# Feed-forward stage: VectorE's statistics and normalising, and GpSimd's closing sum, at other places in their queues; the local-attention loop written out

## The reference

```python
def _layer(x, wqkv, qs, ksc, wo, lg, lb, w1, b1, w2, b2):
    h = shift_token(x)                        # half of the columns from the token before
    q, k, v = jnp.split(h @ wqkv, 3, axis=-1) # 8 heads of 64
    q, k = rotary_xpos(l2norm(q) * qs, l2norm(k) * ksc)
    o = local_attention(q, k, v)              # a window of 128 and the one before it
    x = x + o @ wo
    h = shift_token(x)
    h = (h - mean(h)) / jnp.sqrt(var(h) + 1e-05) * lg + lb
    a, g = jnp.split(h @ w1 + b1, 2, axis=-1) # 682 each
    return x + (a * gelu(g)) @ w2 + b2
...
y = xn
for l in range(2):
    y = _layer(y, wqkv[l], ...)
out = x + s * silu(y)
```

## Time and profile before

| | |
|---|---|
| median of three runs | 1978.15 us (1977.71 to 1978.39) |
| the profiled execution's own time | 1978.07 us |
| its span (first to last instruction) | 1976.2 us |
| busy: PE / PEld / DVE / ACT / POOL | 93% / 66% / 76% / 61% / 50% |
| window phases | about 631 to 1073 us and 1292 to 1725 us |
| feed phases | about 1075 to 1290 us and 1727 to 1976 us |

### The profile page before, as it was taken

The page is one execution under the profiler, slowest core; times in us unless marked ns, Lnnn a source line. Parts: engine busy times, 40 slices in busy tenths (PEclk is TensorE's granted clock), DMA queues, the critical chain, the costliest instruction groups (busy, mean ns, idle before and its releaser), DMA issues. The chain is left out here.

```text
span 1976.2 us, 38537 instructions
## 1 busy us (share of the span) xinstructions
PE 1839.4 (93%) x12768; PEld 1314.2 (66%) x12768; DVE 1502.2 (76%) x4131; ACT 1208.0 (61%) x2523; POOL 988.4 (50%) x801
## 2 busy tenths in 40 slices
PE   6879999999998899999997899979999999789999
PEld 5723333333333687878886788868888888668888
DVE  5778888888881998989996555369999999855654
ACT  3516666666666677777775433447777777644553
POOL 3532223222222777767773433357777777443433
PEclk9969999999998899999998999989999999989999
DMA  6993456456430000000022112110000001232222
GB/s 208 308 194 44 66 68 84 60 74 78 59 44 23 14 28 24 25 28 28 28 74 69 61 57 65 44 35 24 26 27 27 27 27 28 63 117 85 71 69 86
DMA packets 142299, 126.87 MB, mean 64 GB/s; under 512 B 31091, under 2 KB 124719, under 8 KB 141999
## 3 DMA queue, kind: packets, MB, share of 16 engines
q1 hardware_dynamic: 140782, 123.36, 27.2%
q10 hardware_dynamic: 1344, 1.31, 0.2%
HBM read 82.41 MB, written 41.96 MB: 63 GB/s over the span
## 5 line engine op out<-in xcount | busy, mean ns | idle before, releaser
L659 ACT ACTIVATE ca_pr<-ca_pS 128x1024 f32<-128x1024 f32 (+3 forms) x384 | 296.6, 811 | 207.2 <-PE ca_pS L573 166.6
L488 POOL TENSOR_SCALAR_AFFINE_SELECT ca_pr<-ca_pr 128x256 f32<-128x256 f32 x256 | 103.7, 409 | 372.9 <-ACT ca_pr L659 368.8
L687 DVE CUSTOM_DVE_ANT_0 ca_masked<-ca_pR,ca_later 128x256 f32<-128x256 f32 (+3 forms) x512 | 235.9, 485 | 43.2 <-PE ca_pR L549 39.4
L549 PE MATMUL ca_pR<-ca_ks,ca_qs 96*128 96x512 bf16 (+3 forms) x768 | 220.6, 345 | 9.1 <-DVEq L743 5.7
L573 PE MATMUL ca_pS<-ca_qs,ca_ks 98*128 98x512 bf16 (+3 forms) x768 | 184.8, 332 | 10.5 <-issue 5.3
L691 DVE TENSOR_REDUCE ca_mx<-ca_pR 128x1 f32<-128x512 f32 x256 | 175.7, 686 | 24.8 <-PE ca_pR L549 23.0
L549 PEld LDWEIGHTS ca_pR<-ca_ks,ca_qs 96*128 96x128 bf16 x768 | 70.7, 98 | 165.0 <-DVE ca_mx L687 90.6
L909 POOL TENSOR_TENSOR wb_tsn<-wb_qk,wb_tab 128x512 f32<-128x512 f32 x62 | 133.4, 2173 | 71.1 <-DVE wb_pn L1127 71.1
L594 PE MATMUL ca_pO<-ca_pr,ca_va 128*32 128x512 f32 (+3 forms) x1536 | 166.0, 504 | 1.2 <-POOL ca_pr L488 0.8
L909 POOL TENSOR_TENSOR w_tsn<-w_qk,w_tab 128x512 f32<-128x512 f32 x62 | 129.0, 2101 | 76.0 <-DVE w_pn L1127 67.3
L985 ACT ACTIVATE w_pe<-w_sm,w_nmax 128x256 f32<-128x256 f32 (+1 forms) x256 | 123.2, 483 | 66.7 <-DVE w_nmax L1117 66.4
(11 more groups left out here) (293 smaller groups left out, 5417.7 us busy)
## 6 DMA issues: line engine op xcount, KB each, us to landing
QKP<-p_parts SPq DMA_DIRECT2D x32, 384.0 KB, 5.2
ca_qs<-QKP SPq DMA_DIRECT2D x96, 128.0 KB, 6.5
ca_ks<-QKP SPq DMA_DIRECT2D x96, 128.0 KB, 7.0
w_xt<-X SPq DMA_DIRECT2D x64, 128.0 KB, 2.1
X<-w_x SPq DMA_DIRECT2D x64, 128.0 KB, 1.7
f_hh<-X SPq DMA_DIRECT2D x32, 256.0 KB, 6.2
p_xin<-x SPq DMA_DIRECT2D x8, 512.0 KB, 5.7
X<-p_xn SPq DMA_DIRECT2D x8, 512.0 KB, 4.9
```

The source lines that it names most:

```text
L549: pe.matmul(bank[:, 0:w], qs[0:SHIFT_ROW, u, h, i * P:(i + 1) * P], ks[0:SHIFT_ROW, u, h, k0:k0 + w], start=True, stop=True).then_inc(ring ...
L659: act.activation(pr[:, k % 2, pair, :, 0:w], pS[:, pair, :, 0:w], ACT.Exp, scale=CS).then_inc(p_ready, 1)
L687: dve.tensor_tensor_reduce(masked[:, jb % RING, 0:w], pR[jb % RING][:, 0:w], later[:, 512 - w:512], -1.0, BIG, ALU.add, ALU.min, mx[:, i, ...
```

## The change

1. In the window phase `steps` writes out all 32 tiles on every engine; no hardware loop is left.
2. In the feed phase VectorE computes the moments of block s + 2 in three pieces: two `bn_stats` after chunk 0, two after chunk 1, `bn_aggr` after chunk 2. Its normalising moves to `residual`, two instructions ahead of each of the last two results.
3. SP loads the rows of block s + 3 in step s, a block earlier, into the buffer that block s + 1 has left.
4. In the closing phase GpSimd's `gated_sum` moves from the head of a step to behind the second `low`.
5. Block 0 and step 1: ScalarE's high part of w2 comes after block 0 and VectorE's low part after chunk 2 of block 1; TensorE turns block 2 after `up(1)` instead of ahead of it and waits for w2 only there; VectorE's and ScalarE's parts of turning block 2 move with it; block 2's moments come after chunk 4 and its normalising at the end of block 0.

VectorE in layer 0's feed phase, block 0 before, from its chunk 3 to the turned block 2's low part (`f_af` the product, `f_tlo` the turned block's low part, `f_stt`/`f_mv` the moments, `f_hn` the normalised rows, `f_w_lo` w2's low part, `f_ahi` the short chunk's low part).

The core of the diff:

```diff
@@ phase_window
-    def steps(e, step):
-        with e.Fori(0, NW // TPB - 1) as it:
-            for j in range(TPB):
-                step(it * TPB + j, j, it)
-        for j in range(TPB):
-            step(NW - TPB + j, j, NW // TPB - 1)
+    def steps(step):
+        for w in range(NW):
+            step(w, w % TPB, w // TPB)
...
@@ phase_feed, sync
-            sp.wait_ge(S["hn_ready"], ONE + g0 + 1)
-            load_h(sp, F, layer, X, 2, 0)
+            for i in range(2):
+                sp.wait_ge(S["hn_ready"], ONE + g0 + i + 1)
+                load_h(sp, F, layer, X, 2 + i, i)
...
             def step(s, j, it):
-                if within(s, 2) is not None:
-                    sp.wait_ge(S["hn_ready"], ONE + g0 + s + 1)
-                    load_h(sp, F, layer, X, s + 2, j)
+                if within(s, 3) is not None:
+                    sp.wait_ge(S["hn_ready"], ONE + g0 + s + 2)
+                    load_h(sp, F, layer, X, s + 3, 1 - j)
...
@@ phase_feed, gpsimd
             def body(s, j, it):
 
                 for ch in range(WHOLE):
                     low(s, j, ch)
-                    if ch == 1 and within(s, 2) is not None:
+                    if ch == 1 and closing and s >= 3:
+                        gated_sum(s - 3)
+                    if ch == (1 if s else WHOLE - 1) and within(s, 2) is not None:
                         rstd_of(s + 2, j)
...
                 add_b2(s - 1, 1 - j, it - 1 + j)
-                if closing and s >= 3:
+                if closing and s == NS:
                     gated_sum(s - 3)
                 step(s, j, it)
...
@@ phase_feed, scalar
-            def midway():
-                turned(1, 1)
-                act.wait_ge(S["w_loaded"], ONE + (layer + 1) * 4 * 16)
-                act.activation(w2_hi[:, :, :], w2_st[:, :, :], ACT.Copy).then_inc(S["w_hi"], 1)
-
-            gelus(0, 0, midway)
+            gelus(0, 0, lambda: turned(1, 1))
+            act.wait_ge(S["w_loaded"], ONE + (layer + 1) * 4 * 16)
+            act.activation(w2_hi[:, :, :], w2_st[:, :, :], ACT.Copy).then_inc(S["w_hi"], 1)
 
             def step(s, j, it):
-                if within(s, 1) is not None:
+                if s > 1 and within(s, 1) is not None:
                     turned(s + 1, 1 - j)
                 if within(s, 0) is not None:
                     gelus(s, j)
+                if s == 1:
+                    turned(s + 1, 1 - j)
...
@@ phase_feed, vector (residual, body, block 0, step)
                 for n in range(SUP):
+                    if n >= 2 and within(s, 3) is not None:
+                        normalise(s + 3, 1 - j, n - 2)
                     if n == SUP - 1 and within(s, 1) is not None:
                         tail_low(s + 1, 1 - j)
...
-                        if ch == 2:
-                            moments(s + 2, j, it + 1)
-                        elif ch == 3:
-                            normalise(s + 2, j, it + 1)
+                        if ch < 2:
+                            stats(s + 2, j, it + 1, ch)
+                        elif ch == 2:
+                            means(s + 2, j)
+                    if s == 1 and ch == 2:
+                        dve.wait_ge(S["w_hi"], ONE + 4 * layer + 4)
+                        dve.tensor_tensor(w2_lo[:, :, :], w2_st[:, :, :], w2_hi[:, :, :].bitcast(F32), ALU.subtract)\
+                           .then_inc(S["w_split"], 1)
...
-            for ch in range(2, HC):
+            for ch in range(HC):
                 gated(0, 0, ch)
-                if ch == WHOLE - 1:
-                    dve.wait_ge(S["w_hi"], ONE + 4 * layer + 4)
...
-                if ch == 2:
-                    moments(2, 0, 1)
-                elif ch == HC // 2:
+                if ch == HC // 2:
                     lo_of(1, 1)
-                    normalise(2, 0, 1)
+                elif ch == WHOLE - 1:
+                    for half in range(2):
+                        stats(2, 0, 1, half)
+                    means(2, 0)
             tail_low(0, 0)
+            for half in range(2):
+                normalise(2, 0, half)
...
@@ phase_feed, tensor
             up(0, 0, midway)
-            pe.wait_ge(S["w_split"], ONE + 4 * layer + 4)
-            pe.sem_inc(K.passed, 1)
 
             def step(s, j, it):
-                if within(s, 1) is not None:
+                if s > 1 and within(s, 1) is not None:
                     turn(s + 1, 1 - j)
                 if within(s, 0) is not None:
                     up(s, j, lambda: turn_a(s - 2) if closing and s >= 2 else None)
+                    if s == 1:
+                        turn(s + 1, 1 - j)
+                        pe.wait_ge(S["w_split"], ONE + 4 * layer + 4)
```

74 lines of the change are left out of this document (38 added, 36 removed).

## The result

The changed kernel took 1954.89 us, the median of four runs (1951.79 to 1957.08), beside 1977.93 us of the kernel before in the same session. The ratio is 0.9889, with a 95% interval from 0.9873 to 0.9905: 22 us, or 1.1%, faster. The forecast was 1954.5.

What follows compares the result with a forecast made beforehand. TensorE, busy 93% of the span, bounds the kernel, so only its pauses or slow clock can be won. 6.6 + 9.1 + 4.0 + 0.3 + 3.6 = 23.6 us off 1978.07 gives 1954.5 us, range 1950 to 1959 (62%).

Steps and rivals of the forecast that it cites:

- Part 1: Window phase, layer 0: two loop edges each lose 3.29 us when written out, 6.6 us; nothing in layer 1.
- Rival 1: Window phase: loop-edge pauses come back where written-out code jumps or streams; price 6.6, 1961.1 us; 9%.
- rival 5: TensorE's 32 formerly looped tiles: late fetches at 3.29 us each; from 8 on slower, 1981 us; 3%.
- Rival 4: Layer 1's two looped edges: a hidden delay of 3.29 us on each goes too, 1947.9 us; 1%.
- Part 2: Layer 0's feed phase, blocks 2 to 5: the pause in `down`'s third tile goes whole, 9.1 us.
- Part 3: Closing phase, blocks 3 to 6: 28.10 us a block for 29.10 with the sum moved, 4.0 us.
- The margin of the third low part: Closing blocks: low part done 15.3 us after the turning, needed at 17.0 for chunk 4's product; 1.7 spare.
- rival 2: Step 1 or each block: larger or new pauses, part 3 at nothing, part 4 lowest; 1960.1 us; 11%.
- Part 4: Block 0 and step 1: new waits replace old; gains 0.3 us in layer 0, 3.6 in the closing phase.
- the pause ahead of chunk 2: Block 1: TensorE pauses 2.2 us, VectorE being held for most of its low part by GpSimd's bias add.
- What the clock would do: Step 1: slow matmuls behind two pauses over 2.1 us cost 0 to 3.4 us, taken as 2.6.
- rival 3: Step 1: the clock stays up, new pauses being shorter or broken up; 2 x 2.6 more, 1949.3 us; 12%.

Runs made afterwards that it cites:

- loop_out_only: The kernel before with only the window's loops written out, feed-forward phase as it was; 1971.26 us, ratio to before 0.9973.
- pad192: The kernel before with 192 semaphore increments added at the start of TensorE's queue; 1995.62 us, a single run.
- the pads: The kernel before with 64, 128 or 192 semaphore increments added at the start of TensorE's queue; single runs of 1983.59, 1994.52 and 1995.62 us.
- both_back: The changed kernel with VectorE's moments again behind chunk 2 and normalising behind chunk 3, the earlier row load kept; 1968.08 us, ratio to before 0.9945.
- loops_back: The changed kernel with the window's loops put back as loops; 1960.28 us, ratio to before 0.9913.
- sum_back: The changed kernel with GpSimd's closing sum again at the head of its step; 1959.39 us, ratio to before 0.9904.
- turn_mid: The changed kernel with block 2 turned in the middle of block 1's up product rather than after it; 1947.98 us, ratio to before 0.9846.
- bias_later: The changed kernel with GpSimd's bias add of block 0 moved behind its second low part of block 1; 1952.63 us, ratio to before 0.9869.
- pad128: The kernel before with 128 semaphore increments added at the start of TensorE's queue; 1994.52 us, a single run.
- three_moves: The changed kernel with block 2 turned mid block 1, block 0's bias add behind block 1's first low part, woc's low part behind block 0's residual; 1939.26 us.
- pad64: The kernel before with 64 semaphore increments added at the start of TensorE's queue; 1983.59 us, a single run.

## Why the prediction was right, step by step

- **Part 1, 6.6 us.** The two edges gave 2 x (28.15 - 24.85) = 6.6. Rival 1 (the pause moves) and rival 5 (late fetches in written-out code) are out, by the tile ends, by loop_out_only and by the seven packets a round that came without a wait. Why layer 1 gained nothing was open in the prediction; the shifts and the packets show it: its code lay where a round was not fetched again. Rival 4 asked for four edges. The rule of the Trainium skill ("Runtime: NRT & Kernel Launch", section "Instruction fetch mechanics"), that a taken branch outside the buffered window forces a fetch, agrees with the edges that paused. Its window of two pages of 16 KB does not: by it no edge could be free, and the measurement decides, with layer 1 of the kernel before and layer 0 of pad192 free at both edges, though a round is seven packets of 16.4 KB.
- **Part 2, 9.1 us.** 106.77 - 97.71 = 9.06 in the two profiles. The pause went whole, as said. That the size agrees so well is in part luck: the same blocks with the same code take 106.56 to 109.67 us in the five profiles of it (the kernel before, loop_out_only and the pads), according to how late the rows' DMA is, which would make the term 8.9 to 12.0. And the reason given, the normalising gone from between chunks 3 and 4, is only half: the moments' new place alone would have done it. That the earlier load takes the longer pause away is borne out by both_back and by the two groups of profiles.
- **Part 3, 4.0 us.** Measured 3.95 by undoing it. The margin of the third low part, an estimate of 1.7 us, held in all four blocks, which take 28.11 us with no new pause; with that, rival 2 is out.
- **Part 4, 0.3 and 3.6 us.** From block 0's turning to block 3's: -0.38 and 3.95, together 3.6 against 3.9. Step by step: the pause ahead of chunk 2, 2.2 foreseen, 1.96 and 1.94 measured; that in `down(0)`, 2.8 and 3.5 foreseen, 3.04 and 3.65 measured. The list of pauses ahead of the prediction left out the 3.14 us that `down(0)` already waited in the closing phase; as the working started from whole lengths, the sum isn't touched by it. What the clock would do was the weak term. From block 1's turning to block 3's the forecast lengths were 40.8 and 41.5 us, and 40.29 and 42.42 were measured, gains of 0.84 and 2.68. The stretch from block 0's turning to block 1's, whose code on TensorE is the same, added gains of -1.22 and 1.27 us: its granted clock was 0.89 in layer 0 and 0.80 in layer 1 before, and 0.80 and 0.89 after. With phases that begin alike, at 0.89 (the pads for before, loops_back and sum_back for after), the terms are -0.65 and 3.1. In those two kernels layer 0 takes 41.8 us where the forecast, with pauses of nearly the measured size, had 38.2 without the clock: the clock cost some 3.6 there, a little over the bound of 3.4, where 2.6 was taken. In the changed kernel's own layer 0 it cost 2.1, since the pause of 1.96 us was not followed by the slower level (from block 1's turning to block 2's 26.51 us at a granted clock of 1.00, against 28.03 at 0.94 in the closing phase). That is rival 3 in one of four places. So the sum came out right in part because of how the clock fell in this profile.
- **Not in the sum**: 1.3 us more in the window phase of layer 0 and -0.5 in layer 1, 1.2 ahead of the first. They are within what the same code varied by. The terms measured add up to 6.6 + 9.06 + 4.0 + 3.6 = 23.3 us, the profiled execution gained 25.0, and the median of the runs stands 1.9 above that execution. That the median met the forecast to 0.4 us is in part luck; the mechanism of each part is borne out, and the terms are right to about 1 us each in this pair of profiles.
- **Not tested by itself**: the move of w2's two parts out of block 0 and the later turning of block 2 were never undone together. That the wait of 4.29 us for w2's low part is gone is read from the profile after, and what came in its place is tested by turn_mid and bias_later.

## What to carry to other kernels

Ahead of moving work off a late engine, list what in the row of instructions is late and by how much: here two moves each removed the same 1.35 us, and their gains don't add. An instruction moved on GpSimd can hold the VectorE instruction that it lands beside. In these rows that was so for subtractions from SBUF to SBUF and not for products or moments, so look at which neighbour is waited for. The pauses marked "issue" at the loop edges were a matter of the code's place here: look at the instruction queue's packets in the round behind the edge, and shift the code at the queue's start. One shift need not settle it, as it took three here to free layer 0.

## What the runs showed of the hardware

- A hardware loop of this length (seven packets of 16.4 KB a round) ran its second and third rounds without fetching them again at some places of the code, and at others fetched 8 or 9 packets a round, with 2.1 to 2.8 us of pause at each edge. The whole count of the instruction queue follows: 96 where layer 0 pauses, 97 where layer 1 does, 114 where both do.
- A semaphore increment on TensorE's queue took about 0.15 us each: 64 more of them moved TensorE's first matmul by 9.8 us, from 20.56 in pad128 to 30.33 in pad192.
- The bias add slowed what read and wrote SBUF beside it by 1.5 us (0.69 to 2.24 us, 1.73 to 3.20), against its own 2.4. Moments (0.74 us a pair) and products (0.75) were not slowed beside it in three_moves. The Trainium skill ("Advanced Engine Details and Errata", section "Mode Summary") says that the second SBUF port of VectorE is shared with GpSimd and that VectorE's two-port modes and GpSimd's instructions block each other. The four normalising instructions agree, with 3.31 us beside GpSimd's low parts for 1.38. The rows add that subtractions of two SBUF tensors are held as well.
- The clock fell once behind a pause of under 2 us in a block of layer 0. Windows of TensorE in pad64, two blocks of layer 0 (us, busy time of each engine, granted clock, DMA share, GB/s):

```profile
1152.56:1178.56 26.00, 24.64 (x144) 21.41 (x143) 13.59 (x25) 10.44 (x15) 10.06 (x8) 1.00 0.21 61
1178.56:1206.50 27.94, 26.13 (x144) 22.90 (x143) 13.58 (x25) 10.44 (x15) 10.08 (x8) 0.94 0.28 85
```

The second has the same instructions, a pause of 1.81 us in place of 1.35, a granted clock of 0.94, and takes 1.94 us more. The pause is the longer one because the moments ahead of it waited for their rows:

```profile
1189.86 1.41 DVE L1641 BATCH_NORM_STATS2 f_stt<-f_hh 128x6 f32<-128x256 f32 x4 [0.35 <-DMA f_hh<-X]
```

Behind the pause the matmuls of 0.28 us take 0.41. None of the pauses of 1.35 us in layer 0's blocks was followed by such a stretch, as the prediction had it, and neither was one of 1.74 us in loop_out_only, whose block took 26.39 us. Why 1.81 us was and 1.74 wasn't stays open.
